# A second raw w2 buffer, expert loads reordered, and rows centred without rstd in a metaformer layer's kernel

## The reference, cut to what matters

```python
x = x + attention(_ln_c(x))            # rows and columns of a 16x16 image, 8 images, 256 channels
t = tokens(x)                          # 2048 tokens
t = t + _L0_ffn_ref(_ln_t(t), wg, w1, w2)
...
logits = x2d @ wg                      # top-1 gate of 8 experts, capacity C = 256
dispatched = jnp.einsum('szfc,szm->zfcm', dispatch, xr)
h = jax.nn.relu(jnp.einsum('ecm,emh->ech', di, w1))     # w1: 8 x 256 x 1024
eo = jnp.einsum('ech,ehm->ecm', h, w2)                  # w2: 8 x 1024 x 256
out = jnp.einsum('szfc,zfcm->sm', combine, eo)
```

## Time and profile before

| what | us |
|---|---|
| median of 3 runs | 200.94 |
| lowest and highest | 199.15, 201.48 |
| span of the profiled execution | 199.3 |

### The profile page before, as it was taken

How to read it: one execution, slowest core, us unless ns; L and a number is a source line. 1 busy time by engine, 2 the same in 40 slices (tenths; PEclk the granted TensorE clock), 3 DMA queues, 4 the chain that set the end, 5 groups by cost and what they waited for, 6 DMA issues and landing times.

```text
span 199.3 us, 3920 instructions
## 1 busy us (share of the span) xinstructions
PE 179.9 (90%) x1356; PEld 171.8 (86%) x1356; DVE 135.9 (68%) x417; ACT 117.1 (59%) x284; POOL 120.7 (61%) x153
## 2 busy tenths in 40 slices
PE   7599999799999989889996992799999999999990
PEld 7499889699999978669996991799999999999980
DVE  0477999999999997618577718629659486675510
ACT  2347876677875875744788338257493866827000
POOL 3324976195686665575629618648595876918351
PEclk9979999999999999999999999579999999999997
DMA  5799992021131122754961290941926729161010
GB/s 189 217 393 346 266 348 101 33 101 63 58 107 55 58 106 68 246 199 144 311 225 50 61 360 0 312 164 21 355 101 205 269 42 366 71 211 43 3 64 26
DMA packets 23829, 31.67 MB, mean 159 GB/s; under 512 B 2696, under 2 KB 20617, under 8 KB 23808
## 3 DMA queue, kind: packets, MB, share of 16 engines
q1 hardware_dynamic: 21232, 26.32, 40.6%
q0 software_dynamic: 1616, 4.24, 5.9%
q10 hardware_dynamic: 960, 0.85, 1.3%
HBM read 23.02 MB, written 8.55 MB: 158 GB/s over the span
## 4 chain that ended last, share of the span: by engine, by line
PE 51%; DMA 14%; DVE 13%; issue 6%; POOL 6%; ACT 5%; SPq 3%; POOLq 1%; DVEq 0%; ACTq 0%
DMA sl<-slots 5%; PE banks_v L587 5%; PE banks_v L581 5%; PE banks_v L580 5%; PE banks_o L649 4%; DMA wg_sb<-in_L_ffn_wg 3%; PE bank_q L587 3%; DMA w_in_sb<-in_L_ffn_w 3%; PE bank_q L580 3%; PE bank_q L581 3%; ACT w_high L901 2%; PE bank_pT L587 2%; PE bank_pT L580 2%; PE bank_pT L581 2%; POOL w_low L521 2%
## 5 line engine op out<-in xcount | busy, mean ns | idle before, releaser
L521 POOL TENSOR_TENSOR w_low<-w_in_sb,w_high 128x1024 fp32r<-128x1024 f32 x15 | 35.9, 2418 | 10.3 <-ACT w_high L901 10.3
L901 ACT ACTIVATE w_high<-w_in_sb 128x1024 fp32r<-128x1024 f32 x30 | 30.3, 1052 | 6.0 <-DMA w_in_sb<-in_L_ffn_w 6.0
L540 POOL DMA_INDIRECT out<-y,goal x16 | 16.0, 1002 | 18.5 <-issue 8.4
L473 POOL DMA_INDIRECT slots<-row,slot x14 | 14.1, 1010 | 13.6 <-DVE slot L1179 11.1
L1268 DVE TENSOR_TENSOR w_low<-w_in_sb,w_high 128x1024 fp32r<-128x1024 f32 x12 | 18.7, 1591 | 3.0 <-ACT w_high L901 2.8
L649 PE MATMUL banks_o<-v_sb,pT 128*128 128x266 f32 x64 | 16.3, 396 | 0.9 <-ACT pT L867 0.8
L580 PE MATMUL banks_v<-w_high,h_high 128*128 128x256 f32 x64 | 16.0, 287 | 0.0
L1002 ACT ACTIVATE exp_g<-shift_g,rstd_g 128x8 f32<-128x8 f32 x16 | 4.7, 292 | 19.1 <-DVE shift_g L1248 19.1
L581 PE MATMUL banks_v<-w_high,h_low 128*128 128x256 f32 x64 | 15.7, 283 | 0.0
L580 PE MATMUL bank_xT<-xg_high,w_high 128*128 128x256 f32 x32 | 9.3, 310 | 7.0 <-DVE w_low L1268 5.1
L1276 DVE SCALAR_TENSOR_TENSOR h_low<-bank_s,h_high 128x512 fp32r<-128x512 f32 x8 | 5.5, 690 | 14.5 <-ACT h_high L1013 14.5
(11 more groups left out here) (251 smaller groups left out, 658.3 us busy)
## 6 DMA issues: line engine op xcount, KB each, us to landing
w_in_sb<-in_L_ffn_w SPq DMA_DIRECT2D x16, 1024.0 KB, 7.5
sl<-slots SPq DMA_DIRECT2D x9, 266.0 KB, 4.5
slots<-empty SPq DMA_DIRECT2D x8, 266.0 KB, 7.3
out<-row SPq DMA_DIRECT2D x7, 256.0 KB, 2.1
sl<-in_x SPq DMA_DIRECT2D x4, 256.0 KB, 6.1
sl<-in_x SPq DMA_DIRECT2D x2, 512.0 KB, 9.2
table_in<-in_tables SPq DMA_DIRECT2D x1, 292.0 KB, 6.2
w_in_sb<-in_L_conv_Wk SPq DMA_DIRECT2D x1, 256.0 KB, 3.5
```

What stands on the lines that cost most here:

```text
L473: nc.gpsimd.indirect_dma_start(slot_rows, bass.IndirectOffsetOnAxis(ap=slot_of(i)[:, t:t + 1].bitcast(u32), axis=0), row_of(i)[:, t, :], N ...
L521: step = nc.gpsimd.tensor_tensor(w2_low[e % 2][:, half, :], w2_in_sb[:, half, :], w2_high[e % 2][:, half, :].bitcast(f32), ALU.subtract)
L540: nc.gpsimd.indirect_dma_start(out_rows, bass.IndirectOffsetOnAxis(ap=goal[j][:, c:c + 1].bitcast(u32), axis=0), y[j][:, c, :], None, boun ...
L901: nc.scalar.activation(high[e % 2][:, half, :], raw[:, half, :], ACT.Copy).then_inc(ready, 1)
```

## The change

1. A second raw buffer for w2. One tile `vx` takes the place of `xb` and `v_sb` of the attention, and its first 2048 columns are `w2_raw[1]`; even experts use `w2_in_sb`, odd ones `vx`. There is one `w2_in` semaphore for each.
2. SP's order. w1(2) is loaded right after the store of image 5 is issued, ahead of the early slots; w2(1) when the last rows of x2 are ready; w2(2) right after the slot loads; in the loop, w2(e) waits for w2_split of e-1 and no longer of e.
3. Images 6 and 7 and the early slots, and later every expert's slots, are only centred: ACT or DVE adds the negative mean. Because relu(r z) = r relu(z) for r > 0, the factor rstd of a token can be put into the gate: `gate_g` = (1/sum) times rstd, one more DVE instruction per expert. `late_rstd`, `squares` and the `nmr` instructions go, and `gathered` waits for the slots themselves.
4. The order on ACT, DVE and POOL among experts: split_w1(e+2) goes in between the pieces of hidden(e+1), split_w2(e+1) after gathered_T(e+2); at the start, split_w2(1) is taken in two pieces, early, and squares, exps, gathered rows and output_rows(0) change places.

The diff, without the hunks that only name semaphores:

```diff
@@ -165,10 +165,12 @@
         xn = sb("xn", [P, 2, D])
-        xb = [sb(f"xb{j}", [P, 2, VW]) for j in range(2)]
+        vx = sb("vx", [P, 4 * (MW + VW)])
+        xb = [vx[:, 4 * MW + 2 * VW * j:4 * MW + 2 * VW * (j + 1)].rearrange("p (t r) -> p t r", t=2) for j in range(2)]
+        v_sb = [vx[:, 2 * MW * j:2 * MW * (j + 1)].rearrange("p (t r) -> p t r", t=2) for j in range(2)]
+        w2_raw = [w2_in_sb[:, :, :], vx[:, 0:FC * D].rearrange("p (c d) -> p c d", c=FC)]
         xT_high, xT_low = ([sb(f"xT_{n}{j}", [P, DC, TB], f32r) for j in range(2)] for n in ("high", "low"))
         qT_high, qT_low = (sb(f"qT_{n}", [P, DC, TB], f32r) for n in ("high", "low"))
-        v_sb = [sb(f"v_sb{j}", [P, 2, MW]) for j in range(2)]
         s_row, s_col = sb("s_row", [P, 2, P]), sb("s_col", [P, 2, TB])
@@ -187,9 +189,7 @@
         empty = sb("empty", [P, VW])
-        ss_t, var_t, rstd_t, nmr_t = (sb(n, [P, 3, 2]) for n in ("ss_t", "var_t", "rstd_t", "nmr_t"))
-        ss_g, var_g, rstd_g, nmr_g, gsum, gate_g = (sb(n, [P, NT]) for n in ("ss_g", "var_g", "rstd_g", "nmr_g", "gsum", "gate_g"))
+        ss_g, var_g, rstd_g, gsum, ginv, gate_g = (sb(n, [P, NT]) for n in ("ss_g", "var_g", "rstd_g", "gsum", "ginv", "gate_g"))
         lmax_g, shift_g = [sb(f"lmax_g{j}", [P, 2]) for j in range(2)], [sb(f"shift_g{j}", [P, 2, E]) for j in range(2)]
@@ -371,16 +370,21 @@
...
-            for i in range(EARLY):
+            for i in range(EARLY - 1):
                 store_x2(i)
+            sp.wait_ge(x2_ready, 2 * EARLY)
+            sp.dma_start(out_view[:, tiles(EARLY - 1), :], row[1][:, :, 0:D]).then_inc(x2_stored[1], 16)
+            sp.wait_ge(w1_split, 2)
+            sp.dma_start(w1_in_sb[:, :, :], w1_view[2]).then_inc(w1_in, 16)
+            for j in range(2):
+                sp.wait_ge(row_sent[j], 32 * (EARLY // 2))
...
             sp.dma_start(out_view[:, tiles(B - 2), :], row[0][:, :, 0:D]).then_inc(x2_stored[0], 16)
-            sp.wait_ge(early_in, 16)
-            sp.wait_ge(w1_split, 2)
-            sp.dma_start(w1_in_sb[:, :, :], w1_view[2]).then_inc(w1_in, 16)
+            sp.wait_ge(x2_ready, 2 * B)
+            sp.dma_start(w2_raw[1], w2_view[1]).then_inc(w2_in[1], 16)
@@ -394,16 +398,14 @@
                 load_slots(e, 2)
-            sp.wait_ge(w2_split, 1)
-            sp.wait_ge(first_w2_low, 1)
-            sp.dma_start(w2_in_sb[:, :, :], w2_view[1]).then_inc(w2_in, 16)
             sp.sem_inc(y_free, 2)
...
-                sp.wait_ge(w2_split, e)
-                sp.dma_start(w2_in_sb[:, :, :], w2_view[e]).then_inc(w2_in, 16)
+                sp.wait_ge(w2_split, e - 1)
+                if e == 2:
+                    sp.wait_ge(first_w2_low, 1)
+                sp.dma_start(w2_raw[e % 2], w2_view[e]).then_inc(w2_in[e % 2], 16)
                 if e < E - 1:
@@ -498,18 +500,7 @@
...
-            def late_rstd(n, rows):
-                pool.wait_ge(ss_t_ready, n + 1)
-                nc.gpsimd.tensor_scalar(var_t[:, n, :], ss_t[:, n, :], 1.0 / D, EPS_T, ALU.mult, ALU.add).then_inc(var_t_ready, 1)
-                pool.wait_ge(var_t_ready, n + 1)
-                nc.gpsimd.tensor_tensor(rstd_t[:, n, :], var_t[:, n, :], minus_half[:, 0:2], ALU.pow).then_inc(rstd_t_ready, 1)
-                pool.wait_ge(rstd_t_ready, n + 1)
-                nc.gpsimd.tensor_tensor(nmr_t[:, n, :], rows[:, :, COL_MEAN], rstd_t[:, n, :], ALU.mult).then_inc(nmr_t_ready, 1)
-            late_rstd(0, row[0])
-            late_rstd(1, row_last)
-            late_rstd(2, sl_early)
+            pool.wait_ge(early_in, 16)
             scatter_rows(B - 2)
@@ -518,8 +509,9 @@
                     half = slice(part * FC // 2, (part + 1) * FC // 2)
-                    step = nc.gpsimd.tensor_tensor(w2_low[e % 2][:, half, :], w2_in_sb[:, half, :], w2_high[e % 2][:, half, :].bitcast(f32), ALU.subtract)
-                step.then_inc(w2_split, 1)
+                    step = nc.gpsimd.tensor_tensor(w2_low[e % 2][:, half, :], w2_raw[e % 2][:, half, :], w2_high[e % 2][:, half, :].bitcast(f32), ALU.subtract)
+                if part == 1 or e == 0:
+                    step.then_inc(w2_split, 1)
@@ -528,8 +520,6 @@
                 nc.gpsimd.tensor_tensor(rstd_g[:, own], var_g[:, own], minus_half[:, 0:2], ALU.pow).then_inc(rstd_g_ready, 1)
-                pool.wait_ge(rstd_g_ready, turn)
-                nc.gpsimd.tensor_tensor(nmr_g[:, own], sl[:, own, COL_MEAN], rstd_g[:, own], ALU.mult).then_inc(nmr_g_ready, 1)
@@ -544,13 +534,14 @@
             slot_rstd(0, 2)
+            split_w2(1, [0])
             slot_rstd(2, 3)
...
             scatter_y(0)
-            split_w2(1, range(2))
+            split_w2(1, [1])
             slot_rstd(3, 4)
@@ -894,17 +885,17 @@
...
-                act.wait_ge(loaded, 16 * (e + 1))
+                act.wait_ge(*loaded)
                 parts = raw.shape[1] // 2
...
             def split_w1(e, **which):
-                split_w(w1_high, w1_in, w1_in_sb, w1_high_ready, e, **which)
+                split_w(w1_high, (w1_in, 16 * (e + 1)), w1_in_sb, w1_high_ready, e, **which)
             def split_w2(e, **which):
-                split_w(w2_high, w2_in, w2_in_sb, w2_high_ready, e, **which)
+                split_w(w2_high, (w2_in[e % 2], 16 * (e // 2 + 1)), w2_raw[e % 2], w2_high_ready, e, **which)
@@ -946,36 +937,20 @@
...
-            def squares(n, rows, target, t):
-                step = nc.scalar.activation(target[:, t, :], rows[:, t, 0:D], ACT.Square, bias=rows[:, t, COL_MEAN:COL_MEAN + 1],
-                                            accum_out=ss_t[:, n, t:t + 1])
-                if t == 1:
-                    step.then_inc(ss_t_ready, 1)
-            def late_rows(n, rows, target, t):
-                return nc.scalar.activation(target[:, t, :], rows[:, t, 0:D], ACT.Identity, scale=rstd_t[:, n, t:t + 1], bias=nmr_t[:, n, t:t + 1])
+            def centred(rows, target, t):
+                return nc.scalar.activation(target[:, t, :], rows[:, t, 0:D], ACT.Identity, bias=rows[:, t, COL_MEAN:COL_MEAN + 1])
...
                 act.wait_ge(x2_ready, 2 * (B - 2) + t + 1)
-                squares(0, row[0], xn, t)
+                centred(row[0], xn, t).then_inc(xn2_ready, 1)
             for t in range(2):
                 act.wait_ge(x2_ready, 2 * (B - 1) + t + 1)
-                squares(1, row_last, s_col, t)
+                centred(row_last, s_col, t).then_inc(xn2_ready, 1)
             act.dma_start(out_view[:, tiles(B - 1), :], row_last[:, :, 0:D]).then_inc(x2_stored_last, 16)
-            act.wait_ge(nmr_t_ready, 1)
-            for t in range(2):
-                late_rows(0, row[0], xn, t).then_inc(xn2_ready, 1)
             act.wait_ge(early_in, 16)
             for t in range(2):
-                squares(2, sl_early, xs[0], t)
-            act.wait_ge(nmr_t_ready, 2)
-            for t in range(2):
-                late_rows(1, row_last, s_col, t).then_inc(xn2_ready, 1)
-            act.wait_ge(nmr_t_ready, 3)
-            for t in range(2):
-                step = late_rows(2, sl_early, xs[0], t)
+                step = centred(sl_early, xs[0], t)
             step.then_inc(xs0_ready, 1)
@@ -1013,29 +988,34 @@
...
-            hidden(0, range(4))
+            hidden(0, [0, 1])
+            split_w2(1, which=[0])
+            hidden(0, [2, 3])
+            split_w1(2, which=[0])
             slot_squares(1, 1)
-            split_w1(2, which=[0])
+            gathered_T(1)
             slot_squares(0, 2)
+            split_w1(2, which=[1])
             slot_exps(1, 1)
-            gathered_T(1)
             slot_exps(0, 2)
-            split_w1(2, which=[1])
+            hidden(1, [0, 1])
             slot_squares(2, 3)
-            hidden(1, [0, 1])
-            split_w2(1)
             hidden(1, [2, 3])
             gathered_T(2)
+            split_w2(1, which=[1])
             slot_squares(3, 4)
             for e in range(1, E - 1):
-                if e + 1 < E:
-                    slot_exps(e + 1, e + 2)
-                hidden(e + 1, [0, 1])
-                split_w2(e + 1)
+                hidden(e + 1, [0])
+                if e + 2 < E:
+                    split_w1(e + 2, which=[0])
+                slot_exps(e + 1, e + 2)
+                hidden(e + 1, [1])
+                if e + 2 < E:
+                    split_w1(e + 2, which=[1])
                 hidden(e + 1, [2, 3])
                     gathered_T(e + 2)
-                    split_w1(e + 2)
+                split_w2(e + 1)
                 if e + 3 < E:
@@ -1249,12 +1229,12 @@
...
-            def gathered(e, turn):
-                dve.wait_ge(nmr_g_ready, turn)
+            def gathered(e):
+                dve.wait_ge(*slots_landed(e))
                 for t in range(2):
                     r = 2 * e + t
-                    step = nc.vector.tensor_scalar(xs[e % 2][:, t, :], sl[:, r, 0:D], rstd_g[:, r:r + 1], nmr_g[:, r:r + 1], ALU.mult, ALU.add)
```

(32 more changed lines are left out.)

2 lines of the change are left out of this document (1 added, 1 removed).

## The result

The changed kernel takes 192.06 us in the median (191.21 to 193.34, 4 runs) against 201.09 (199.15 to 201.48, 4 runs): ratio 0.9584, 95% interval 0.9508 to 0.966. It is 9.0 us faster. The forecast was 193.5. The profiled execution took 191.21 us with a span of 189.4, so 1.8 us lie around the span.

A forecast was written before the change was run, and what follows sets the result against it. The prediction took PE (90% busy) to bound the kernel, with one large pause before layer 3. Terms: 199.3 - 8.1 - 0.3 + 1.9 = 192.8 us of span, 194.4 by the median; forecast between, 193.5, range 190.5 to 197.5.

The forecast's parts named there:

- Buffer and SP's order: Before layer 3: w1(3), issued earlier, lands in time, so PE's pause and the slow clock go; gain 8.1 us.
- Handover: At the start of hidden layer 0: centring only lets it start 0.85 us earlier, bounded by zero and 1.4.
- Reordering at expert 1: Before layer 2: DVE and POOL race, xg_low(2) +0.5 or -0.4 us against 108.89, taken +0.3; handover gain mostly given back.
- Steady stage: Middle experts: one more DVE multiplication (0.2 us) each; the loop through y's scatter slips; no stall, at bound 0 to 3.
- The slip of the w1 loads: Loop through POOL and y's scatter: 25.7 us per two experts against PE's 23.9, slipping 1.8 each turn, spare about 0.4 by layer 7.
- rival 2: The loop through y's scatter becomes the bound: layers 6 and 7 wait for w1, 2 to 4 us more, 196.5; chance 0.14.
- PE doesn't see it: Steady stage: the moved w1 and w2 work on ACT and DVE is hidden where a hidden layer lies between, 12 us a period.
- The end: Before expert 7's output: PE waits 1.0 us for POOL's split_w2(7), 2.2 or more with the slip; taken as 1.9.
- The scale: Profiled span put at the runs' lower end: 192.8 of span, 194.4 by the median, forecast between at 193.5.
- rival 1: Small things fall well: DVE first at 101, no slip, 1.0 at the end; 191.0 of span, 191.8 on forecast's scale; chance 0.24.
- Rivals 3 and 4: First: layer 3 or expert_out(1) waits for POOL's second w2(1) piece; 6 us late, about 200; chance 0.07. Second: see rival 4.
- rival 4: Before layer 2: slots landing 7 us later hold DVE at gathered(2), PE idles, clock halves; 202.6, or 203.4 scaled; chance 0.05.

The follow-up runs named there:

- e1: The changed kernel with SP's old wait put back before w2(2), which also holds w1(3): 202.37 us, ratio 1.0083.
- e3: The kernel before with only the second raw buffer and SP's new order: 193.92 us, ratio 0.966.
- e2: The kernel before with the centring alone (one raw buffer, old orders): 200.77 us, ratio 0.9986.
- e6: The changed kernel with ACT's rounding of w2(7) put back between the pieces of hidden layer 7: 192.7 us, ratio 0.957.
- e5: The changed kernel with each expert's gate and goal made after the first h_low instead of ahead of y: 192.48 us, ratio 0.958.
- e4: The kernel before with second buffer, SP's order and centring, but the old order of ACT, DVE and POOL: 194.84 us, ratio 0.9714.
- e7: The changed kernel with the edits of both e5 and e6: 191.34 us, ratio 0.9539.
- e11: The changed kernel with e7's edits and POOL's first half of w2_low(1) moved before the small rstd instructions: 191.12 us, ratio 0.9537.

## Why the prediction was right, and where it wasn't

- **Buffer and SP's order.** Right in mechanism and size. w1(3) was to be issued at 102 to 106 and is at 101.00 (102.05 on the scale of before, with the 1.05 of the start added); 8.1 us were forecast, 8.07 came. e1 takes the gain away with one wait, e3 gets 6.8 us with nothing else.
- **Handover.** 0.85 forecast, 1.08 measured (1.07 in e2), within the bound of 1.4. The early load of w1(2) didn't delay the early slots.
- **Reordering at expert 1: the mis-sized term.** I had the slots in SBUF at 100.7 and ACT's half at 101.0, and took PE to pause 2 to 3 us, with +0.3 or so for handover and layer 2 together. On the scale of before (1.05 added) `gathered(2)` began at 99.65 and w1_low(2) at 100.80, the pause was 0.79, and the two terms gave 1.79 us. What I had wrong is who holds PE there: I followed DVE's queue to an xg_low(2) at 108.4, and it ended at 107.1 on that scale, hidden behind ACT's rounding of the same rows, which sets the 0.79. That DVE and POOL race here was right; e6 shows the lost race, dearer than my two ends (0.9 us apart): 3.2 us with the low clock. I had left out that `gathered` itself can be held, and named it only as the page's rule.
- **Steady stage.** No wait of PE from 112 to 177 us, as forecast. The slip of the w1 loads is real: ACT begins to round w1(3) at 107.87 and w1(7) at 158.45, 50.58 later, where four periods of 11.95 are 47.80, so 2.8 us have slipped. It makes PE wait nowhere before 177; rival 2 didn't come. e5, which lets y's scatter go 2.4 us earlier (1.9 without its earlier start) and gains nothing, says the same. What I hadn't seen is that e4's queue would be hit so hard without the new order: the step "PE doesn't see it" is true because of the order, not beside it.
- **The end: mis-sized too.** 1.9 forecast, 0.8 of wait and 0.9 of time measured. I took the slip to come on top of the structural 1.0; the two run beside each other and e5, e6 and e7 show that they end together; without both, in e7 and e11, 0.94 and 0.96 of time go. In e1 the wait is 1.8.
- **The scale.** I read one dip in the row of PE's clock; the 7 in the slice of 10 to 15 us is another, the slow start, worth the 1.05 us above. And I put the profiled execution at the low end of the runs. All later runs show 1.8 us around the span (191.21 with 189.4), so it was at 201.1, the median. The terms gave 6.5 us of span and 8.9 came, without the start's luck: by the median they would have given 194.4, and the forecast, placed 0.9 below that for a reason that didn't hold, hid a part of their error. The result lies between the forecast and rival 1 (191.8), nearer to rival 1. Of its conditions the profile shows two, DVE first and about 1.0 at the end, and not the third, no slip.
- Rivals 3 and 4 didn't come. The condition of rival 4, slots 6.5 us late, was far away; e6 with slots about 1 us late is its small form.

## What to carry to other kernels

Where a load is chained to the far end of another engine's work by a single raw buffer, follow the issue queue back to that wait first: here one `wait_ge` decided most of 9 us. Look for short elementwise instructions of DVE that fall beside long ones of POOL: move them to where POOL is idle, but only after asking what else has the same date, since with two equal causes neither edit shows a gain alone. Don't book a gain ahead of a stall before the stall and the queue behind it are gone: in e4 the earlier start was lost there, and in e2 no median showed it. And before pricing a queue on one engine, look whether another engine's work covers it, as ACT's did before layer 2.
